# State scan stage: the scan's input stays in SBUF and is spread by a float32 product of 32 rows

## What is computed

```python
xz = x @ W_in
x_e, z = jnp.split(xz, 2, axis=-1)
xc = silu(causal_conv(x_e, conv_w) + conv_b)
x_dbl = xc @ W_x
delta_r, Bmat, Cmat = split(x_dbl, (64, 16, 16))
delta = jax.nn.softplus(delta_r @ W_dt + b_dt)
A = -jnp.exp(A_log)
deltaA = jnp.exp(delta[..., None] * A[None, None])
deltaB_x = delta[..., None] * Bmat[:, :, None, :] * xc[..., None]
# H[t] = deltaA[t] * H[t-1] + deltaB_x[t]
y = jnp.einsum('bldn,bln->bld', H, Cmat) + xc * D
y = (y * silu(z)) @ W_out
```

## Time and profile before

| | |
|---|---|
| three runs | 1981.05, 1988.71, 1990.2 us |
| span of the profiled execution, first to last instruction | 1883.9 us |
| state scan stage in it, first item to last scan | 1103.4 to 1594.1 us |
| mean granted TensorE clock | 0.844 of 2.4 GHz |
| busy in the span: TensorE, VectorE, ScalarE, GpSimd | 73%, 68%, 44%, 46% |

### The profile page before, as it was taken

The page is one execution under the profiler, slowest core; times in us unless marked ns, Lnnn a source line. Parts: engine busy times, 40 slices in busy tenths (PEclk is TensorE's granted clock), DMA queues, the critical chain, the costliest instruction groups (busy, mean ns, idle before and its releaser), DMA issues. The chain is left out here.

```text
span 1883.9 us, 29315 instructions
## 1 busy us (share of the span) xinstructions
PE 1376.5 (73%) x8975; PEld 714.5 (38%) x8976; DVE 1286.4 (68%) x2984; ACT 833.7 (44%) x1181; POOL 866.1 (46%) x763
## 2 busy tenths in 40 slices
PE   4459999999999798683995857586666544592992
PEld 2113333333333576552894322132221101362991
DVE  4568898988884255673332179999999998671433
ACT  3405666666667211121453458457475232121551
POOL 3401111121211434375565237867868665573662
PEclk9658999999999688797997778798788766796996
DMA  4721111211141566442333286985867763723335
GB/s 129 243 80 51 43 62 38 61 45 52 51 71 37 81 93 96 134 105 87 83 91 93 60 227 152 244 198 150 223 151 193 190 153 78 181 92 110 92 91 150
DMA packets 219597, 214.96 MB, mean 114 GB/s; under 512 B 49504, under 2 KB 188739, under 8 KB 217155
## 3 DMA queue, kind: packets, MB, share of 16 engines
q1 hardware_dynamic: 197454, 184.90, 39.5%
q0 software_dynamic: 9216, 19.02, 3.2%
q10 hardware_dynamic: 12800, 9.46, 1.7%
HBM read 149.46 MB, written 63.37 MB: 113 GB/s over the span
## 5 line engine op out<-in xcount | busy, mean ns | idle before, releaser
L806 ACT ACTIVATE attn_prob<-attn_ps_cols 128x1024 f32<-128x1024 f32 (+1 forms) x320 | 290.5, 940 | 224.1 <-PE attn_ps_cols L682 222.7
L2340 POOL TENSOR_TENSOR ssm_hc<-ssm_h,ssm_cb 128x1024 f32<-128x1024 f32 x128 | 302.5, 2364 | 169.2 <-DVE ssm_h L2323 124.4
L2323 DVE TENSOR_TENSOR_SCAN ssm_h<-ssm_decay,ssm_ps_u 128x1024 f32<-128x1024 f32 x128 | 292.7, 2287 | 17.6 <-DVE ssm_ps_u L2318 0.5
L832 POOL TENSOR_SCALAR_AFFINE_SELECT attn_prob<-attn_prob 128x512 f32<-128x512 f32 x128 | 81.2, 634 | 421.4 <-ACT attn_prob L806 421.3
L714 DVE CUSTOM_DVE_ANT_0 attn_ps_rows<-attn_ps_rows,const_mask_rows 128x384 f32<-128x384 f32 (+3 forms) x512 | 235.5, 528 | 39.6 <-PE attn_ps_rows L649 39.6
L649 PE MATMUL attn_ps_rows<-attn_ks,attn_qs 72*128 72x512 bf16 (+3 forms) x768 | 225.7, 346 | 42.7 <-DMA attn_qs<-parts_dram 29.2
L2311 ACT ACTIVATE ssm_decay<-ssm_wide,ssm_aneg 128x1024 f32<-128x1024 f32 x128 | 146.0, 1146 | 181.5 <-DVE ssm_h L2323 121.0
L2274 PE MATMUL ssm_ps_u<-ssm_stack,ssm_spread 96*128 96x512 bf16 x256 | 96.2, 465 | 177.3 <-DVE ssm_h L2323 172.3
L682 PE MATMUL attn_ps_cols<-attn_qs,attn_ks 75*128 75x512 bf16 (+3 forms) x768 | 191.8, 330 | 4.8 <-DMA attn_qs<-attn_nrows 4.0
L701 PE MATMUL attn_ps_o<-attn_prob,attn_vw 128*32 128x512 f32 (+3 forms) x1536 | 164.3, 500 | 0.3 <-POOL attn_prob L832 0.3
L719 DVE TENSOR_REDUCE attn_nm<-attn_ps_rows 128x1 f32<-128x512 f32 x256 | 157.6, 684 | 5.8 <-PE attn_ps_rows L649 5.8
(11 more groups left out here) (331 smaller groups left out, 2473.1 us busy)
## 6 DMA issues: line engine op xcount, KB each, us to landing
ssm_wide<-delta_dram SPq DMA_DIRECT2D x128, 512.0 KB, 6.6
attn_ks<-parts_dram SPq DMA_DIRECT2D x48, 192.0 KB
attn_qs<-parts_dram SPq DMA_DIRECT2D x48, 192.0 KB
parts_dram<-proj_parts SPq DMA_DIRECT2D x8, 768.0 KB, 3.8
ffn1e_x<-ex_dram SPq DMA_DIRECT2D x40, 130.0 KB, 2.3
ffn2e_x<-ex_dram SPq DMA_DIRECT2D x40, 130.0 KB, 2.3
split_dram<-ssm_parts SPq DMA_DIRECT2D x6, 768.0 KB, 4.3
ssm_stack<-split_dram SPq DMA_DIRECT2D x18, 256.0 KB, 4.2
```

The lines of the kernel that those rows point to most:

```text
L806: nc.scalar.activation(prob[u % RING][:, heads[0]:heads[-1] + 1, 0:w], ps_cols[s % 2][:].rearrange("p b (x q) -> p (b x) q", x=len(heads) ...
L2323: nc.vector.tensor_tensor_scan(h[t % H_RING][:], decay[t % DECAY_RING][:], ps_u[t % 2][:], 0.0, ALU.mult, ALU.add).then_inc(scan_done, 1)
L2340: nc.gpsimd.tensor_tensor(hc[:, t % HC_RING, :], h[t % H_RING][:], cb[b % 2][:], ALU.mult).then_inc(hc_done, 1)
```

## The change

u is no longer split. GpSimd (VectorE in the opening) writes u once, in float32, into `u[b % 2]` of 128 partitions x 2 x 1024, and `spread_u` multiplies the 32 partitions of the item's quad with the same 32 rows of a float32 `spread`. `high`, `rest`, `middle`, `low`, `store_split` and `stack_u` go, with their buffers, semaphores and memory. In the opening, item 0's spread is moved ahead of `c` and `turn` of half 2, decays 0 and 1 are moved ahead on ScalarE, and four `widen` loads are issued in one row.

```diff
-SROWS_U = PARTS * 32
-LOADS = PARTS * 16
-            ("dt0", 0), ("dt1", 0), ("z0", 1), ("z1", 1), ("dr", 1), ("dt0", 1), ("dt1", 1), ("b", 0), ("c", 0), ("b", 1), ("c", 1), ("turn", 2)]
+            ("dt0", 0), ("dt1", 0), ("z0", 1), ("z1", 1), ("dr", 1), ("dt0", 1), ("dt1", 1), ("b", 0), ("b", 1), ("c", 0), ("c", 1), ("turn", 2)]
-POOL_AT = {0: [("sum", 1)], 2: [("rstd", 1)], 13: [("u", 0)], 15: [("rest", 0)], 17: [("low", 0)], 19: [("u", 1)], 21: [("rest", 1)],
-           23: [("low", 1)], 25: [("sum", 2)], 27: [("rstd", 2)]}
+POOL_AT = {0: [("sum", 1)], 2: [("rstd", 1)], 13: [("u", 0)], 19: [("u", 1)],
+           25: [("sum", 2)], 27: [("rstd", 2)]}
...
-        spread = m.sb("spread", [SROWS_U, SETS, STATES, CPI], BF16)
+        spread = m.sb("spread", [P, SETS, STATES, CPI])
-        parts = m.sb("parts", [P, PARTS, CH, UNIT], BF16)
-        stack = [m.sb(f"stack{k}", [SROWS_U, CH, QUADS, T], BF16) for k in range(2)]
+        u = [m.sb(f"u{k}", [P, CH, T]) for k in range(2)]
...
+            if n >= 4:
+                eng.wait_ge(u_spread, (n // 2 - 1) * PER_BATCH)
             eng.sem_inc(passed, 1)
-            ops.tensor_tensor(dtx_of(n)[:, at], delta_of(n)[:, at], gated[n // 2 % 2][:, at, cols(n)], ALU.mult).then_inc(u_ready, 1)
+            ops.tensor_tensor(u[n // 2 % 2][:, at, cols(n)], delta_of(n)[:, at], gated[n // 2 % 2][:, at, cols(n)], ALU.mult).then_inc(u_ready, 1)
...
             b, ch, j, q = of_item(t)
-            if t == 0:
-                for k in range(2):
-                    nc.tensor.wait_ge(stack_begun[k], LOADS)
-            elif t % PER_BATCH == 0 or t == PER_HALF:
-                for k in range(2):
-                    nc.tensor.wait_ge(stacked[k], (b + 1) * LOADS)
+            if t % PER_BATCH == 0 or t == PER_HALF:
+                nc.tensor.wait_ge(u_ready, did(2 * b + 1, ch))
             if t >= 2:
                 nc.tensor.wait_ge(scan_done, t - 1)
             for at in (0, UNIT):
-                done = nc.tensor.matmul(ps_u[t % 2][:, at:at + UNIT], spread[:, j].rearrange("p n c -> p (n c)"),
-                                        stack[b % 2][:, ch, q, at:at + UNIT], start=True, stop=True)
+                done = nc.tensor.matmul(ps_u[t % 2][:, at:at + UNIT], spread[32 * q:32 * q + 32, j].rearrange("p n c -> p (n c)"),
+                                        u[b % 2][32 * q:32 * q + 32, ch, at:at + UNIT], start=True, stop=True)
...
-                for part, n in PE_FIRST[13:]:
+                for part, n in PE_FIRST[13:18]:
                     prepare_pe(part, n)
-                pe.wait_ge(a_ready, 2)
                 spread_u(0)
+                for part, n in PE_FIRST[18:]:
+                    prepare_pe(part, n)
...
-                prepare_act(act, "b", 0)
                 for n in range(2):
-                    prepare_act(act, "high", n, 0)
-                prepare_act(act, "c", 0)
+                    prepare_act(act, "b", n)
+                act.wait_ge(a_ready, 2)
+                make_decay(act, 0)
...
+                    prepare_act(act, "c", n)
+                make_decay(act, 1)
                 prepare_act(act, "norm", 2)
-                for n in range(2):
-                    prepare_act(act, "middle", n, 1)
                 prepare_act(act, "turn", 2)
```

More of the change, by code:

```diff
@@ L1932 @@
           27: [("stats", 2)]}
-POOL_AT = {0: [("sum", 1)], 2: [("rstd", 1)], 13: [("u", 0)], 15: [("rest", 0)], 17: [("low", 0)], 19: [("u", 1)], 21: [("rest", 1)],
-           23: [("low", 1)], 25: [("sum", 2)], 27: [("rstd", 2)]}
+POOL_AT = {0: [("sum", 1)], 2: [("rstd", 1)], 13: [("u", 0)], 19: [("u", 1)],
+           25: [("sum", 2)], 27: [("rstd", 2)]}
 SP_AT = {0: [("residual", 0), ("residual", 1)], 2: [("keep", 1)], 4: [("load", 2)], 6: [("store", 0), ("store", 1)], 14: [("delta", 0)],
-         19: [("delta", 1), ("split", 0)], 20: [("stack", 0)], 25: [("split", 1)], 26: [("stack", 1)], 27: [("keep", 2)], 28: [("load", 3)]}
+         19: [("delta", 1)], 27: [("keep", 2)], 28: [("load", 3)]}
 def of_phase(table, phase, s):
@@ L2019, in scan @@
         abs_ready, exp_ready, ln_ready, delta_ready, u_ready = (m.sem(n) for n in ("abs", "exp", "ln", "delta", "u"))
-        delta_stored, split_stored, stacked = m.pair("delta_st"), m.pair("split_st"), m.pair("stacked")
-        delta_begun, split_begun, stack_begun = m.pair("delta_be"), m.pair("split_be"), m.pair("stack_be")
-        high_ready, rest_ready, middle_ready, low_ready = (m.sem(n) for n in ("high", "rest", "middle", "low"))
+        delta_stored, delta_begun = m.pair("delta_st"), m.pair("delta_be")
         wide_loaded = [m.sem(f"wide{s}") for s in range(WIDE_RING)]
@@ L2143, in prepare_act @@
                 return
[L2144 to L2154, removed]
             act.wait_ge(bank_done, turn_of(part, n) + 1)
@@ L2253, in prepare_pool @@
                 make_rstd(pool, n)
-            elif part == "u":
+            else:
                 make_u(pool, nc.gpsimd, n)
[L2256 to L2259, removed]
         def spread_u(t):
             b, ch, j, q = of_item(t)
-            if t == 0:
-                for k in range(2):
-                    nc.tensor.wait_ge(stack_begun[k], LOADS)
-            elif t % PER_BATCH == 0 or t == PER_HALF:
-                for k in range(2):
-                    nc.tensor.wait_ge(stacked[k], (b + 1) * LOADS)
+            if t % PER_BATCH == 0 or t == PER_HALF:
+                nc.tensor.wait_ge(u_ready, did(2 * b + 1, ch))
             if t >= 2:
@@ L2445, in _ @@
                     store_delta(sp, n, 0)
[L2446 to L2452 removed]
+                for t in range(WIDE_RING):
                     widen(sp, t)
@@ L2455, in _ @@
                     store_delta(sp, n, 1)
-                for n in range(2):
-                    store_split(sp, n, 1)
                 def parts(phase, s):
@@ L2468, in parts @@
                             keep_x(sp, n)
-                        elif part == "delta":
+                        else:
                             store_delta(sp, n)
-                        elif part == "split":
-                            store_split(sp, n)
-                        else:
-                            stack_u(sp, n)
                 for t in range(ITEMS):
@@ L2636, in _ @@
                 pool.wait_ge(filled, 3)
-                for r in range(PARTS):
+                for r in range(QUADS):
                     nc.gpsimd.affine_select(out=spread[:], in_=spread[:], compare_op=ALU.not_equal, fill=1.0, base=-32 * r,
```

72 lines of the change are left out of this document (9 added, 63 removed), and 2 rows, old and new, of the table ACT_AT.

## The result

The changed kernel takes 2109.1 us, the median of four runs (2097.0 to 2113.4), the one before beside it 1985.2: ratio 1.0586, 95% interval 1.0546 to 1.0627, so 5.9% or 116 us slower (the plain difference of the two medians is 124 us). The forecast was 2048 with a range from 2004 to 2104; the measured time lies just above it.

A forecast was written before the change was run, and what follows sets the result against it. VectorE was taken to bound the state scan throughout; longer TensorE spreads would add 18 + 15 + 12 + 14 = 59 us, the opening 0. On the run median of 1988.7 this gave 2048 us, range 2004 to 2104.

The forecast's parts named there:

- the price of a spread: An item's float32 spread on TensorE: 1.8 us at 2.4 GHz, 3.5 at 1.2, including 0.1 for changing array shapes.
- (1): Items 0 to 12 of three batches: TensorE's 56.1 us at full clock exceed VectorE's 50.0, +18 us in all.
- (2): Items 13 to 22: TensorE 44.8 us at clock 0.80 or 51.1 at 0.70; +5 taken, three times, +15 us.
- (4): Last batch, 116.1 us: eight groups of spreads and sums at mixed clock, 1.7 us each, +14 us.
- my alternative of two lost tails an item: Two tails of 0.17 us lost per item instead of 0.1: each batch's first thirteen items 3 us later.
- (3): Items 23 to 31, mostly spreads and sums: +1.7 us per four items at mixed clock, +4 three times, +12 us.
- The argument by the earlier trace: TensorE busy with few-row products was granted 0.50, so its clock stays where it was or a little lower.
- rival (a): Clock rises to 2.4 GHz with TensorE's busy share; only items 0 to 12 lose, +18, 2007 us; chance 0.18.
- Rival (b): Clock falls further as longer spreads push 128-row work apart: +170, 2159 us; chance 0.10 for more than half way there.
- +115: Upper bound of the forecast's slowdown, giving the range's high end of 2104 us.
- The opening: Stage start: scan 0 8.7 us earlier, head start gone by item 2; bounds 8.7 gained and 2 lost, taken 0.
- Removed parts: Parts of u, stores and loads removed from ScalarE and GpSimd, lighter DMA queues: 0 outside the opening, hidden by VectorE.

The follow-up runs named there:

- The 128-row run: Changed kernel with each spread as two float32 products of all 128 rows, zeros outside the quad's 32 rows: 2009.3 us, ratio to before 1.0119.
- the second: Profile of the changed kernel, unedited, run again beside the one before in another session: 2114.4 us, ratio 1.0642.
- the experiment: Changed kernel with only the opening put back into its old order (spread 0, decays 0 and 1 later): 2096.3 us, ratio 1.0576.
- The one-pass run: Changed kernel with u and spread matrix in bfloat16, 32 rows, middle and low parts of u left out: 1977.3 us, ratio 0.9972.

## Why the prediction was right and wrong

The direction and the mechanism were right in the main: with 32-row float32 spreads TensorE becomes the bound in items 0 to 12 and holds VectorE up in the others, and its clock stays mixed. The size was half of what came, 59 us against 116. Three steps of the sum were too low: the price of a spread, the full clock in (1), and the length of (2) to (4), into which I put no idle time of TensorE.

**The spread's price** was the first term that was mis-sized. I took 1.8 us at 2.4 GHz, with 0.1 for the change of shape, by the reading that little of it shows in the 1.92 us of the sums. That row could not show it, since the sums always stand between other shapes, and part of the price lies in the neighbour: with 128 rows the spreads on either side of the sums hold 1.81 and 1.82 us, and 1.71 between `conv` and the output products. The new spread costs 1.98 us an item by the 13.20 against 12.42 us, 2.1 where each stands between 128-row products. The trace before had a better row, the 64-row `dt` between two spreads of 96 rows:

```profile
1291.00 1.98 PE L2110 MATMUL ssm_ps_m<-ssm_xn,ssm_wdt 64*128 64x512 f32 x4
1292.91 0.60 PE L2274 MATMUL ssm_ps_u<-ssm_stack,ssm_spread 96*128 96x512 bf16 x2
```

It holds the engine 1.91 us start to start, where four records make 1.72: 0.19 for one change, as the 32-row spread then did. The Trainium skill (TensorEngine Tiling (Array Packing), Key Properties) says that a change of tiling mode drains the engine; the 0.39 us a pair agree, and my alternative of two lost tails an item (0.34) was near. I weighed it at 3 us more for each first stretch; it was 2.3 (13 x 0.18).

**(1), +6 forecast, +12.5 measured.** The 128-row run separates the terms, in batch 1: the passes at full clock give 54.4 - 50.0 = +4.4 (my sum had 55.1 without any shape changes); shape changes 13 x 0.26 = +3.4; what is left of 62.6, +4.8, I put down to the clock, 0.91 instead of the full one that I had kept. Holding it at full was the step that failed: the spreads are nearly half of the work there (13 x 1.98 of 57 us), and with 64 and 128 rows in them the same stretch is granted 0.94 and 1.00.

**(2), +5 forecast, +13.6 measured.** The bounds were +1 and +8; the first profile is also the lucky one here, the second has +15 to +18. At a clock of 0.73 TensorE's busy time in batch 1 came to 51.1 us, what I had worked out for 0.70: I should have taken that bound. Another 4.2 us in which it is idle came on top, which no term of mine held: I took the longer of the two engines' sums for the length, and where they wait for each other in turn the stretch is longer than either. With 128 rows it is +1.3.

**(3) and (4), +4 and +14 forecast, +5.7 and +19.9 measured.** The clock was as forecast (0.66 and 0.65; some spreads at 2.4 GHz, the sums at 1.2). What fills the time was not. I gave each four items three slow spreads, a fast one and the sums, 15.9 us of work without a gap. They took 17: TensorE worked for 13.2 us (7.25 + 3.57 + 2.35), less than I had summed, and stood idle for 3.5 to 4.0 until a scan ended. In the last batch it is idle for 26.5 of 137.3 us. Spread and scan wait for each other in turn, as in (2), and a comparison of two sums leaves that out.

**The clock.** The argument by the earlier trace rows, that few rows do not bring 2.4 GHz however busy the engine is, held in the last batch: 110.8 of 139.2 us busy with 0.65, against 85.4 of 121.9 with 0.96 for full rows (which also have fewer changes of shape). Where the spreads are under half of an unbroken stream, in (1), it still gets 0.91. The rule of the Trainium skill (TensorE: Matmul & The Clock Gate, What's actually happening), taken as one of busy time alone, would have given rival (a), 2007 us; the measurement decides against it for 32 rows. What (a) priced did come, at 2009 us, when the rows were made 128. Rival (b), the clock falling further, came in part: in (2) from 0.80 to 0.73, in (3) and (4) by 0.03 only. The time lies at the +115 from which I had counted (b), the rest of the way there by the terms above. That +115 was half way between the forecast and (b), and no sum of the forecast's own upper ends: with +8 for each of (2), the only upper end I had worked out, they come to +68. That the result lies no further above the range than it does is luck.

**The opening, 0 forecast.** Scan 0 came 9.0 us earlier (8.7 forecast), item 2 at the old place. The step was right by number. That the old order would start item 2 at the same place with the new spread, as I expected in the experiment, was wrong: it starts it 6.8 us earlier.

**Removed parts, 0 forecast.** The one-pass run bears it out: everything removed, the old time, and in batch 1, away from the opening, 126.3 us against 126.7.

**The sum.** Putting the change on the median of the runs and not on the profiled span was right, though not for the reason given ahead of it: the stage differs by 117.1, the medians by 124 in one session and 126 in another, with intervals that reach down to 108.

VectorE's waits were to go to some 60 us and went to 110.1, which is the same errors again.

## What to carry to other kernels

Price a product on TensorE by the row of its own shape at the clock that its surroundings will be granted, not by the best row: here 32 rows in float32 cost as much as 128 do, a change of shape on both sides, and part of the clock of what stands near them. Where a small product feeds a chain, padding its matrix with zeros to 128 rows can be the cheaper form: here it gave back 96 of 117 us for the same result. And when the engine that you load was not the bound, set its sum against the bound's time at both clocks, take the upper one where the new work is what lowers the clock, and add the waits where the two engines take turns.

## What was not expected of the hardware

- The granted clock went with the rows of the products, not with the busy time alone: in the last batch 0.65 with 32 rows, 0.70 with 64, 0.96 with 128 (the last without the spread's changes of shape).
- Adding 22 products of 128 rows, over 23 us of work, to an engine that was busy 80% of the time made the batch 0.3 us longer; adding sixteen made it 3 us shorter.
- Two items' spreads of neighbouring quads, ready together, run side by side: eight records in 2.23 us where four take 1.98 (1692.84 above). In the view above it comes about behind the sums.
- The same kernel in two sessions, on two chips: 1983 and 1889 us, with the scan stage 578.7 and 576.8 us long in its two profiles, a short and a long one.
- The same instructions within one execution: items 13 to 22 take 55.0, 55.4 and 58.8 us in batches 0 to 2.
